# Half the first query products, POOL's weight subtractions behind the gate, and the first batch's sums behind the last expert rows

## The reference

```
A1, A2 = Q1 K1^T / sqrt(128), Q2 K2^T / sqrt(128)
attn = softmax(A1) - lam * softmax(A2)
O = rms_norm(attn @ V) * rms_scale * (1 - LAMBDA_INIT)
x = layernorm(X + O Wo^T)
probs = softmax(x @ gate_w)                # 8 experts
top_p, top_idx = top_k(probs^T, 256)       # every expert takes 256 tokens of a batch
y = gelu(x[top_idx] @ w1) @ w2 * top_p
out = layernorm(x + scatter_add(y))
```

## Time and profile before

| | |
|---|---|
| median of 3 runs (lowest to highest) | 931.21 us (930.83 to 931.35) |
| profiled execution: own time, span | 930.3 us, 928.6 us |
| PE busy, granted clock over the span | 873.8 us (94%), 0.98 |
| DVE, ACT, POOL busy | 708.2, 748.7, 643.3 us |
| chain that ended last: PE, DVE, POOL | 81%, 6%, 4% |

### The profile page before, as it was taken

How to read it: one execution, slowest core, us unless ns; L and a number is a source line. 1 busy time by engine, 2 the same in 40 slices (tenths; PEclk the granted TensorE clock), 3 DMA queues, 4 the chain that set the end, 5 groups by cost and what they waited for, 6 DMA issues and landing times.

```text
span 928.6 us, 15029 instructions
## 1 busy us (share of the span) xinstructions
PE 873.8 (94%) x4654; PEld 736.2 (79%) x4656; DVE 708.2 (76%) x1209; ACT 748.7 (81%) x1454; POOL 643.3 (69%) x1031
## 2 busy tenths in 40 slices
PE   6899999999999999999999999999999999876964
PEld 4678888888888888888888888888888887766953
DVE  5777777777777777777777768789998886597755
ACT  4888888888888888888888888888888897766642
POOL 3766767676776767676778766777676778696851
PEclk9999999999999999999999999999999999879997
DMA  5010001000000000000101110101000011331241
GB/s 165 1 29 1 29 1 29 1 27 4 7 23 1 29 1 29 0 30 1 30 1 42 34 30 3 29 3 30 1 17 2 9 32 42 102 85 30 46 72 46
DMA packets 42271, 25.44 MB, mean 27 GB/s; under 512 B 5408, under 2 KB 40256, under 8 KB 42192
## 3 DMA queue, kind: packets, MB, share of 16 engines
q1 hardware_dynamic: 38864, 21.20, 7.9%
q0 software_dynamic: 3328, 3.28, 2.2%
HBM read 20.14 MB, written 4.33 MB: 26 GB/s over the span
## 4 chain that ended last, share of the span: by engine, by line
PE 81%; DVE 6%; POOL 4%; issue 3%; ACT 3%; DMA 1%; another core or an unknown queue 0%; SPq 0%; POOLq 0%; DVEq 0%; ACTq 0%
PE t_ps L1483 11%; PE ring_a L1446 6%; PE ring_a L1448 6%; PE ring_a L1447 6%; PE ring_b L1446 6%; PE ring_b L1448 6%; PE ring_b L1447 6%; PE u_ps L1446 6%; PE u_ps L1448 6%; PE u_ps L1447 6%; PE o_ps L1446 3%; PE o_ps L1447 2%; PE o_ps L1448 2%; PE x_ps L1446 1%; PE x_ps L1448 1%
## 5 line engine op out<-in xcount | busy, mean ns | idle before, releaser
L587 POOL TENSOR_TENSOR attn<-prob 128x1024 f32<-128x1024 f32 x128 | 306.9, 2398 | 177.8 <-ACT prob L741 169.3
L982 DVE TENSOR_TENSOR at_lo<-t_ps,at_hi 128x512 fp32r<-128x512 f32 x253 | 173.9, 687 | 91.7 <-ACT at_hi L724 91.4
L975 DVE TENSOR_REDUCE negmax<-ring_a 128x1 f32<-128x1024 f32 x128 | 156.7, 1224 | 62.6 <-PE ring_a L1448 60.6
L724 ACT ACTIVATE at_hi<-t_ps 128x512 fp32r<-128x512 f32 x253 | 151.7, 600 | 40.1 <-PE t_ps L1483 39.3
L975 DVE TENSOR_REDUCE negmax<-ring_b 128x1 f32<-128x1024 f32 x128 | 156.0, 1219 | 1.7 <-PE ring_b L1448 0.9
L1483 PE MATMUL t_ps<-ident,attn 128*128 128x128 f32 x1012 | 152.1, 272 | 3.7 <-DVE at_lo L982 3.5
L741 ACT ACTIVATE prob<-prob,coef 128x1024 f32<-128x1024 f32 x128 | 147.6, 1153 | 2.6 <-POOL coef L549 2.6
L1483 PEld LDWEIGHTS t_ps<-ident,attn 128*128 128x128 f32 x1012 | 124.9, 140 | 28.9 <-DVE at_lo L982 8.3
L735 ACT ACTIVATE prob<-ring_a,negmax 128x1024 f32<-128x1024 f32 x128 | 142.9, 1116 | 5.8 <-DVE negmax L975 5.2
L735 ACT ACTIVATE prob<-ring_b,negmax 128x1024 f32<-128x1024 f32 x128 | 142.6, 1114 | 1.2 <-DVE negmax L975 1.2
L1446 PE MATMUL ring_b<-xt_hi,q_hi 128*128 128x512 f32 x256 | 111.5, 435 | 2.3 <-ACT prob L735 2.3
(11 more groups left out here) (440 smaller groups left out, 1834.8 us busy)
## 6 DMA issues: line engine op xcount, KB each, us to landing
attn<-in_L_ffn_w SPq DMA_DIRECT2D x12, 256.0 KB, 3.3
wq_s<-in_L_attn_Wq SPq DMA_DIRECT2D x16, 128.0 KB, 2.5
wk_s<-in_L_attn_Wk SPq DMA_DIRECT2D x16, 128.0 KB, 2.6
wv_s<-in_L_attn_Wv SPq DMA_DIRECT2D x16, 128.0 KB, 2.1
wvt_s<-in_L_attn_Wv_T SPq DMA_DIRECT2D x16, 128.0 KB, 2.5
wot_s<-in_L_attn_Wo_T SPq DMA_DIRECT2D x16, 128.0 KB, 2.7
xres<-in_L_attn_X SPq DMA_DIRECT2D x2, 512.0 KB, 7.7
xg_dram<-xres SPq DMA_DIRECT2D x2, 512.0 KB, 3.7
```

Of the source, the lines that this page charges most:

```text
L587: pool.tensor_tensor(attn[:, t % AB, :], prob[:, t % 2, 1, :], prob[:, t % 2, 0, :], ALU.add).then_inc(attn_ready, 1)
L724: act.activation(at_hi[:, g % 2, half * GT:(half + 1) * GT, c], t_bank(t, half)[:, :].rearrange("p (k q) -> p k q", q=P), ACT.Copy).then_i ...
L975: dve.tensor_reduce(negmax[:, par, m:m + 1], ring[m][:, :], axis=AX.X, op=ALU.max, negate=True).then_inc(negmax_ready, 1)
L982: dve.tensor_tensor(at_lo[:, g % 2, k, c], t_bank(t, half)[:, :].rearrange("p (k q) -> p k q", q=P), at_hi[:, g % 2, k, c].bitcast(F32), A ...
```

## The change

- **Start.** Only the first two of the four first query products stand ahead of the loop on TensorE; the other two follow tile 0's scores, with their `q_round` and `q_part` at tiles 1 and 2. `xk_hi` of batch b is copied behind the row maxima of tile b, `xk_lo` subtracted at POOL's tiles 0 and 1. Batch 1's X^T is loaded behind the next head's weights, into `xg0`, and split at tiles 20 to 32.
- **Gate of batch 1.** POOL waits for `ln_done` 4 instead of `gate_step` 11 ahead of its weight subtractions. `gate_rep` is cut in two, and each half of `row_transposes` waits for its own. Both halves of the gate products stand ahead of `rows_in(0)`, `ln_vars(1, 0)` ahead of the second `x1t_copy`.
- **Scatters.** `scatter(2)` stands ahead of the gathers of batch 1's rows.
- **End.** `add_parts` and its means stand behind `ffn(33)` on VectorE, ScalarE's squares of batch 0 behind its last `ffn`, `ln_end(2)` behind `add_mixed`. Batch 1's output goes out in four parts.

The diff, its unchanged lines cut:

```
@@ -84,6 +84,7 @@
     M_NORM, M_REP, M_SCAN, M_CHOOSE, M_PICK, M_SPREAD, M_IDX = 91, 92, 118, 120, 122, 123, (125, 126)
+    G_XTHI, G_XTLO = (20, 28), (24, 32)
@@ -165,8 +166,8 @@
-        xt_raw = [prob[:, 0, 0, :], attn[:, 3, :]]
         xg0 = sb("xg0", [P, E * CT * XW])
+        xt_raw = [prob[:, 0, 0, :], xg0[:, 0:N]]
@@ -404,7 +405,6 @@
                 sp.dma_start(xt_raw[0][:, c * NC:(c + 1) * NC], XT[0][:, c * NC:(c + 1) * NC]).then_inc(xt_in[c], 16)
-            sp.dma_start(xt_raw[1], XT[1]).then_inc(xt_in[2], 16)
@@ -412,6 +412,7 @@
             load_qk(1)
+            sp.dma_start(xt_raw[1], XT[1]).then_inc(xt_in[2], 16)
@@ -451,12 +452,13 @@
             for b in range(B):
-                for h in range(2):
-                    s = slice(h * GT, (h + 1) * GT)
+                parts = 2 * (b + 1)
+                for h in range(parts):
+                    s = slice(h * QT // parts, (h + 1) * QT // parts)
...
                                  x1[:, b * QT:(b + 1) * QT, :][:, s, :]).then_inc(out_done, 16)
-            sp.wait_ge(out_done, 32 * B)
+            sp.wait_ge(out_done, 16 * (2 + 4))
@@ -490,7 +492,8 @@
-            for b in range(B):
+            def xk_lower(b):
+
@@ -582,8 +585,6 @@
                 pool.wait_ge(scaled_ready, t + 1)
-                if t == 3:
-                    pool.wait_ge(xt_split, 4)
@@ -634,8 +635,12 @@
             for G in range(TILES):
+                if G == 0:
+                    xk_lower(0)
...
                     factor(G - LAG_C)
+                if G == 1:
+                    xk_lower(1)
@@ -668,7 +673,7 @@
             gather_rows(4, 1)
-            pool.wait_ge(gate_step, 11)
+            pool.wait_ge(ln_done, 4)
@@ -678,13 +683,13 @@
             pool.iota(tok_row, pattern=[[1, N]], base=0, channel_multiplier=0).then_inc(row_ready, 1)
-            for q in range(2):
+            for q in range(3):
...
                     gather_rows(q, k)
-            for q in range(2, E):
+            for q in range(3, E):
@@ -766,8 +771,10 @@
                 act.wait_ge(gate_step, 6 * b + 5)
-                act.activation(pr_rep[b].rearrange("p (t e j) -> p t e j", e=E, j=REP),
-                               pr[:, b].unsqueeze(3).broadcast_to([P, QT, E, REP]), ACT.Copy).then_inc(gate_step, 1)
+                for h in range(2):
+                    act.activation(pr_rep[b][:, h * NC:(h + 1) * NC].rearrange("p (t e j) -> p t e j", e=E, j=REP),
+                                   pr[:, b, h * GT:(h + 1) * GT].unsqueeze(3).broadcast_to([P, GT, E, REP]),
+                                   ACT.Copy).then_inc(gate_step, 1)
@@ -823,21 +830,22 @@
-            for c in range(NCH):
-                for m in range(2):
-                    q_round(0, m, c, (x_ps, t_ps, u_ps, o_ps)[2 * c + m][:, :])
+            for m in range(2):
+                q_round(0, m, 0, (x_ps, t_ps)[m][:, :])
...
                 k, s = (G - 1) // QT, (G - 1) % QT
-                if G == 1:
-                    for c in range(NCH):
-                        act.wait_ge(xt_in[2], 16)
-                        act.activation(xt_hi[:, N + c * NC:N + (c + 1) * NC], xt_raw[1][:, c * NC:(c + 1) * NC],
-                                       ACT.Copy).then_inc(xt_hi_done, 1)
+                if G in G_XTHI:
+                    c = G_XTHI.index(G)
+                    act.wait_ge(xt_in[2], 16)
+                    act.activation(xt_hi[:, N + c * NC:N + (c + 1) * NC], xt_raw[1][:, c * NC:(c + 1) * NC],
+                                   ACT.Copy).then_inc(xt_hi_done, 1)
...
                     exponential(G - LAG_E, 1)
+                if G in (1, 2):
+                    q_round(0, G - 1, 1, (u_ps, o_ps)[G - 1][:, :])
@@ -902,9 +910,8 @@
                 ffn(n)
-                if n == 2 * JOBS:
-                    for c in range(QT):
-                        ln_squares(2, c)
+            for c in range(QT):
+                ln_squares(2, c)
@@ -1044,7 +1051,8 @@
                                                ALU.add, ALU.mult)
-                last_x.then_inc(ln_done, 1)
+                    if c % GT == GT - 1 or (n == 3 and c % 2 == 1):
+                        last_x.then_inc(ln_done, 1)
@@ -1282,15 +1290,16 @@
                 xt_lower(n)
-            for c in range(NCH):
-                for m in range(2):
-                    q_part(0, m, c, (x_ps, t_ps, u_ps, o_ps)[2 * c + m][:, :])
+            for m in range(2):
+                q_part(0, m, 0, (x_ps, t_ps)[m][:, :])
...
                               ALU.mult).then_inc(rms_ready, 1)
-            for b in range(B):
+
+            def xk_round(b):
+
@@ -1300,15 +1309,16 @@
                 row_max(G, 0)
+                if G in (1, 2):
+                    q_part(0, G - 1, 1, (u_ps, o_ps)[G - 1][:, :])
...
                     wp_parts(k)
-                if G == 1:
-                    for n in range(NCH, 2 * NCH):
-                        xt_lower(n)
+                if G in G_XTLO:
+                    xt_lower(NCH + G_XTLO.index(G))
@@ -1333,6 +1343,8 @@
                 row_max(G, 1)
+                if G < B:
+                    xk_round(G)
@@ -1383,8 +1395,8 @@
             ln_means(1, 1)
+            ln_vars(1, 0)
             x1t_copy(1)
-            ln_vars(1, 0)
@@ -1417,21 +1429,20 @@
                     one_hots((n - 2 * E) // 2)
-                if n in (2 * JOBS - 3, 2 * JOBS - 1):
-                    h = (n - 2 * JOBS + 3) // 2
-                    add_parts(h)
-                    ln_means(2, h)
             ffn(2 * JOBS + 1)
+            for h in range(2):
+                add_parts(h)
+                ln_means(2, h)
+            ffn(2 * JOBS + 3)
...
             ln_vars(2, 1)
-            for h in range(2):
-                ln_end(2, h)
-            ffn(2 * JOBS + 3)
...
                 ln_means(3, h)
+            for h in range(2):
+                ln_end(2, h)
@@ -1534,8 +1545,7 @@
-                if h == 0:
-                    pe.wait_ge(gate_step, 6 * (b + 1))
+                pe.wait_ge(gate_step, 6 + 6 * b + b * h)
@@ -1578,10 +1588,10 @@
             pe.wait_ge(m_split, 1)
-            for c in range(NCH):
-                pe.wait_ge(xt_split, c + 1)
-                for m in range(2):
-                    q_product(0, m, c, (x_ps, t_ps, u_ps, o_ps)[2 * c + m][:, :])
+            pe.wait_ge(xt_split, 1)
+            for m in range(2):
+                q_product(0, m, 0, (x_ps, t_ps)[m][:, :])
+            pe.wait_ge(xt_split, NCH)
@@ -1612,10 +1622,13 @@
                 scores(G, 1, 1)
+                if G == 0:
+                    for m in range(2):
+                        q_product(0, m, 1, (u_ps, o_ps)[m][:, :])
...
                 if exists(r):
-                    if r == 0:
-                        pe.wait_ge(xk_split, B)
+                    if r % BT == 0:
+                        pe.wait_ge(xk_split, r // BT + 1)
@@ -1793,8 +1806,8 @@
             gate(1, range(GT))
+            gate(1, range(GT, QT))
             rows_in(0)
-            gate(1, range(GT, QT))
```

## The result

Over four runs each, the changed kernel took 922.98 us (922.28 to 923.65) and the kernel before 931.02 us (929.46 to 931.35): ratio 0.9916, 95% interval 0.9902 to 0.9929. The forecast was 924.6. The profiled execution took 922.28 us, span 920.5. A later group of runs, on one chip, had the same kernel at 1.0022 times the kernel before of that group (1.0010 to 1.0034). The third and fourth group of experiments show where the difference arises.

The account below looks back on a forecast made before the run. TensorE was taken to bound 59 to 790 us, so time could move only before and behind. +1.5 + 2.5 + 0.4 - 11.5 + 0.5 = -6.6 us gave 924.6 by the median; own range 922.5 to 927, with rivals 921.3 to 928.3.

Parts of the forecast that it names:

- start, at the last combine: Attention ramp: POOL's second `xk_lower` delays `combine(0)` by 1.5 us, carried to every tile: +1.5 us (+0.7 to +2.7).
- XT subtractions: Tiles 20 to 32: later XT[1] load and roundings cost nothing beside TensorE's work; without that cover 2.4 us.
- POOL's subtractions, likewise: Gate of batch 1: subtractions wait for the normalisations, start at 814.9 instead of 812.03, POOL's queue 2.9 us later.
- first gather, likewise: Batch 2's experts: queue 2.9 later plus scatter 2's 3.9, less 4.3 of idle time absorbed: +2.5 us (0 to 4).
- start, gathers and clock, at output 12: Ahead of the tail: start +1.5, gathers +2.5, and +0.4 for slower products after TensorE's longer idle time.
- stall: Tail: with `add_parts` behind output 14's work, output 15 is scaled at 904.3 instead of 915.86: -11.5 us.
- end: After output 15: `ln_end(2)` ahead of the last normalisations costs 1.0, the smaller last store saves 0.5: net +0.5 us.
- One sign of being right: Tail: no wait of VectorE over 1 us between outputs 12 and 14.
- the start gains: Rival at the attention ramp: `combine(0)` isn't held, so -2.4 instead of +1.5, 920.7 us; chance 0.13.
- the sums land too late: Rival in the tail: sums land after 903.7, VectorE waits ahead of output 15; 6 us late gives 927.6; chance 0.07.
- lost phase of the attention stage: Rival: after the altered ramp TensorE waits once a tile; at 0.1 us a tile 936.6 us; chance 0.04.
- Normalisations that stay slow: Rival at batch 1's gate: `ln_end` takes 6.11 instead of 2.13, first gather 4 us later, 928.6 us; chance 0.06.

Follow-up runs that it names:

- third and fourth group: Third: changed kernel unaltered 933.38 us (1.0022), mended start again 930.89 (0.9998). Fourth: kernel before unaltered 932.57 (0.9994), altered tail with the mended start 929.92 (0.9957).
- the tail alone: Kernel before with only the order of the tail changed (sums, ScalarE's squares, last normalisations later; scatter 2 behind the gathers): 921.78 us, ratio 0.9909.
- 1.0032 alone: Kernel before with only the start of the change, nothing behind it: 932.87 us, ratio 1.0032.
- mended start: Changed kernel with both X roundings and subtractions ahead of tile 0, XT subtractions at tiles 23 and 31: 931.43 us (0.9974), again 930.89 (0.9998).
- altered tail with the mended start: Kernel before with the altered tail (output in four parts) and the mended start, gate and scatters as before: 929.92 us, ratio 0.9957.
- at tile 40: Changed kernel with the second batch's X rounding and POOL's subtraction moved from tile 1 to tile 40: 923.06 us, ratio 0.9930.
- second to fourth group: Second: four kernels, mended start, no start part, scatter 2 back, POOL's wait back: 931.43 to 935.50 us. Third and fourth: two kernels each, 929.92 to 933.38.

## Why the prediction came out as it did

By its own steps, in us against the kernel before, for the pair of the first measurement:

| step | forecast | measured |
|---|---|---|
| start, at the last combine | +1.5 | +1.3 (+0.66 at tile 0, the rest at tiles 24 and 32) |
| XT subtractions | 0 | +0.5 at tile 24, +0.5 at tile 32, part given back |
| eight normalisations | 2.1 | 2.14 |
| first count, without the start's shift | -2.3 | -2.8 |
| POOL's subtractions, likewise | +2.9 | +2.2 |
| first gather, likewise | +2.5 | +1.6 |
| start, gathers and clock, at output 12 | +4.4 | +3.0 (894.17 against 891.13) |
| stall | -11.5 | -11.7 (-8.7 at output 15, less the 3.0) |
| end | +0.5 | +0.6 |
| sum | -6.6 | -8.1 (spans 928.6 and 920.5) |

**The mechanism** held in each part: the start lost by POOL's order, POOL's queue was late by the wait, its idle time took in scatter 2, the stall and the slow products behind it went, and the tail alone gave 0.9909. The 1.5 us by which the sum was off lie nearly all in one term, the shift of output 12. Most of its miss began at `gate_max`: forecast 0.9 late, measured 811.64 - 810.16 - 1.3 = 0.2, so POOL's queue was 2.2 instead of 2.9 late, and the gathers 1.6 instead of 2.5. What is left for the idle time's cost is 0.1 (3.0 - 1.3 - 1.6) instead of 0.4. One sign of being right did not come: VectorE waited for over 1 us between outputs 12 and 14 (1.24 us, ahead of output 14 at 902.58).

**One step was wrong:** that the later XT roundings "cost nothing". The cover was argued from a tile's whole time, "beside TensorE's own work"; what counts is what stands behind the instruction in VectorE's queue, and here a remainder that TensorE waits for stood there. At tiles 23 and 31 the steps are gone. **Another was right with less than it looks:** `combine(0)` at +1.5 was read as +0.66 in the first pair, but the inputs landed 0.64 us earlier in that execution (first product at 4.92 instead of 5.56). The means over the traces, 23.9 for the old start and 25.3 for the changed one, give +1.5; at the last combine they give +2.2.

**The rivals.** That the start gains is refuted for the change (1.0032 alone). In its mended form the last combine does come 2 us earlier; that form was not timed alone. That the sums land too late did not happen, but with scatters and gate left in place it does, for 2.45 us; so scatter 2 brings the sums earlier and the gathers later, and by the sheet (134.9 against 135.8) it and the gate part together are worth 0.9 us in these single traces. The lost phase of the attention stage did not occur (TensorE lacks 2.6 us of 731 in place of 2.1). Normalisations that stay slow did not occur either, and POOL's wait is shown to be why.

**What the forecast had no case for** is that the stall was slack. It priced 8.7 us of waiting as lost, from one trace, and never asked what else could fill it. In three of the four groups, each on its own chip, something did. The changed kernel itself was timed in one of these three, at 933.38 us and 1.0022: slightly slower than before, by about what its start costs, and outside the forecast's range. That the first measurement met no late ends was the forecast's luck.

The lowest ratio beside late ends is that of the altered tail with the mended start, which leaves out gate, scatters and XT places of the change: 0.9957. Without late ends it was not run; from the parts (921.78 less 784.1 - 782.1) it would be an estimated 919.8.

## What to carry to other kernels

A wait in one trace is worth what it costs only where nothing upstream of it varies: before removing a stall, ask which other delays it absorbs, and measure on more than one chip. A rounding or subtraction that seems free in a stage with room is paid by the instruction right behind it in its queue, and moving it moves the price too: at tile 40 it took back the 2 us gained, while in true idle time (12.63 to 18.53 us in the mended start) no later tile showed a step for it. In a ramp that is a loop over engines, look for the engine that closes the loop; earlier inputs only make the others wait.

## What the runs showed of the hardware

Between about 862 and 882 us, in all eight traces of the second to fourth group and in none of the six others, TensorE's products released their waiters late, the latest of each trace 6.7 to 11.2 us after its recorded start, while POOL issued gathers and scatters at its usual pace. In the changed kernel's trace the granted clock is 1.00 from 866 to 879 us, where the latest ends are; the loads of instructions stand at the same places in both traces of this kernel (863.39 and 866.52 us in the first, 863.66 and 866.48 in the other). So neither explains it. The Trainium skill (TensorE: Matmul & The Clock Gate, Part 1) warns that recorded clock events are at times unreliable on this chip; no run here shows whether that is so in this case. The recording itself is a rival that nothing here tests. The eight traces hold fewer semaphore events than the six others, 6592 to 6689 against 7070 to 7104, with the same number of products (4654 or 4656). Most of the missing ones tell of a DMA's landing, and so the profile gives no time from issue to landing for any scatter in the eight, where it gives medians of 3.2 to 3.4 us in the six. Against this rival, such events are missing between 790 and 800 us too, where nothing is seen to be late. That it is a property of the chips is argued from the groups, each on one chip, and the cause stays open.

A VectorE copy of 1024 columns took 0.68 us alone and 2.87 beside a POOL instruction of 2.40; eight normalisations of 128 columns 2.14 alone and 6.12 beside 5.10 us of POOL's. Row maxima read from PSUM kept their 1.2 us beside the same POOL instructions.
